# Four stages on one core: planes and pixels fetched from SBUF, first features made earlier, stores issued by SP, loops written out

## The reference

```python
x = x + _L0_conv_ref(_gn(x), w, b)        # 3x3 convolution, quantised
x = x + _L1_conv_ref(_gn(x), w1, w2)      # Fourier layer, 32x32 modes
x = x + _L2_conv_ref(_gn(x), cw, cb)      # 5x5 depthwise, filters pooled from the image
x = x + _L3_conv_ref(_gn(x), cw, ...)     # the layer that the change is about
```

```python
patches = _unfold(x, oh, ow)                        # 3x3 patches, (B, C, 3, 3, 128, 128)
x1 = patches.max(axis=1); x2 = patches.max(axis=2); x3 = patches.max(axis=3)
y = relu(bn(einsum('bihw,oi->bohw', concat([x1, x2, x3], 1), conv_w)))
out = mean(patches * y, over the 9 patch positions) # then pixel shuffle by 2
```

## Time and profile before

| | us |
|---|---|
| median of 3 runs | 3263.21 (3260.43 to 3278.74) |
| the profiled execution: time, span | 3277.86, 3276.0 |
| busy: PE, DVE, POOL, ACT | 2748.8, 2654.4, 1831.2, 1817.2 |
| fourth stage of image 0: first and last product on DVE | 589.61 to 931.04 |

### The profile page before, as it was taken

How to read it: one execution, slowest core, us unless ns; L and a number is a source line. 1 busy time by engine, 2 the same in 40 slices (tenths; PEclk the granted TensorE clock), 3 DMA queues, 4 the chain that set the end, 5 groups by cost and what they waited for, 6 DMA issues and landing times. The chain is left out here.

```text
span 3276.0 us, 45677 instructions
## 1 busy us (share of the span) xinstructions
PE 2748.8 (84%) x12765; PEld 2135.7 (65%) x12765; DVE 2654.4 (81%) x3575; ACT 1817.2 (55%) x2351; POOL 1831.2 (56%) x1296
## 2 busy tenths in 40 slices
PE   0087698899989779799989769889998977979998
PEld 0036586777747658577765658677775765857776
DVE  8986987788884888688888598778888489868887
ACT  7753655656552655566655265566655265556654
POOL 2013272799940446299990327279994044629998
PEclk9998899999997889899999689999999788989999
DMA  6732002899840200789880200289985020078984
GB/s 252 251 102 71 1 0 69 228 223 227 188 155 3 68 0 0 189 217 228 208 212 35 71 1 0 69 226 224 226 188 155 2 69 0 0 189 216 229 209 113
DMA packets 116199, 419.22 MB, mean 128 GB/s; under 512 B 16565, under 2 KB 30693, under 8 KB 105354
## 3 DMA queue, kind: packets, MB, share of 16 engines
q1 hardware_dynamic: 96058, 374.65, 44.5%
q10 hardware_dynamic: 18432, 38.54, 3.3%
q0 software_dynamic: 1616, 4.90, 0.5%
HBM read 340.57 MB, written 75.26 MB: 127 GB/s over the span
## 5 line engine op out<-in xcount | busy, mean ns | idle before, releaser
L920 POOL TENSOR_TENSOR work<-work 128x512 f32<-128x512 f32 x960 | 1283.3, 1342 | 411.0 <-DVE work L1340 310.4
L575 PE MATMUL psum<-workr,w 128*128 128x512 f32 (+1 forms) x5760 | 1366.0, 397 | 67.2 <-ACT workr L792 50.6
L575 PEld LDWEIGHTS psum<-workr,w 128*128 128x128 f32 (+1 forms) x5760 | 1085.9, 189 | 346.6 <-issue 51.4
L1331 DVE SCALAR_TENSOR_TENSOR work<-psum,work 128x512 f32<-128x512 f32 x1152 | 738.2, 679 | 34.0 <-POOL work L920 21.4
L544 PE MATMUL psum<-workr 128*128 128x512 f32 x2304 | 550.9, 401 | 21.5 <-DVE workr L1228 21.5
L894 POOL TENSOR_TENSOR work<-img 128x520 f32 (+1 forms) x256 | 387.7, 1545 | 283.7 <-DVE workr L1200 254.3
L544 PEld LDWEIGHTS psum<-workr 128*128 128x128 f32 x2304 | 439.7, 191 | 134.2 <-issue 24.7
L884 POOL TENSOR_TENSOR work<-work 128x1024 f32<-128x1024 f32 x40 | 112.9, 2856 | 479.1 <-DVE work L1113 479.1
L772 ACT CAST workr<-psum 128x650 fp32r<-128x650 f32 x128 | 90.0, 703 | 419.2 <-DVE psum L1307 419.2
L440 PE MATMUL psum<-work,taps 128*128 x1152 | 261.6, 391 | 44.4 <-DVE work L1064 44.4
L1304 DVE TENSOR_TENSOR psum<-psum,work 128x650 f32<-128x650 f32 x128 | 107.9, 843 | 208.4 <-ACT psum L765 208.2
(11 more groups left out here) (188 smaller groups left out, 3506.1 us busy)
## 6 DMA issues: line engine op xcount, KB each, us to landing
work<-gn_dram SPq DMA_DIRECT2D x256, 585.0 KB, 10.6
work<-gn_dram SPq DMA_DIRECT2D x256, 146.2 KB, 3.9
work<-gn_dram SPq DMA_DIRECT2D x128, 292.5 KB, 4.8
work<-in_x SPq DMA_DIRECT2D x16, 2048.0 KB, 7.3
img<-in_x SPq DMA_DIRECT2D x32, 1024.0 KB, 11.4
work<-in_mixw SPq DMA_DIRECT2D x64, 512.0 KB, 5.3
out_x<-work ACTq DMA_DIRECT2D x120, 256.0 KB, 6.2
gn_dram<-img SPq DMA_DIRECT2D x24, 1040.0 KB, 16.6
```

The lines of the kernel that those rows point to most:

```text
L575: mm = T.matmul(bank(m % 6), w5[wt][0:kr, P * n:P * n + P], ft[0:kr], start=(i == 0), stop=(i == 4))
L920: G.tensor_tensor(acc_t[v], acc_t[v], pd_t[(9 * v + n) % 6], ALU.add).then_inc(s_acc, 1)
L1331: V.scalar_tensor_tensor(out=tile4(pd_t[m % 6]), in0=tile4(psum[:, m % 6, :]), scalar=0.0, in1=rv[:, q, y0:y0 + RT, x0:x0 + WO], op0=ALU.m ...
```

## The change

- `gn_dram` and `store_rows` go. Planes and pixels are read from `img` in SBUF. A DMA takes one range of partitions on each side there, so the pixels are 16 DMAs of 32 partitions instead of 4 (`s_inr` counts 256 a pair instead of 64).
- SP issues the stores of tiles 0 to 29 in `load_next`: that of tile `2i` after the planes and ahead of maxima and pixels, that of tile `2i + 1` after the pixels. ACT's `store` goes. POOL still stores the last two tiles.
- The first tile's front part is made among the 32 reductions of `L1295` (DVE after reductions 20, 21 and 24, ACT ahead of its copies of the maxima), and PE's first products start ahead of the maxima; the transposed maxima go to PSUM bank 5 instead of 0.
- Every `Fori` inside an image (PE, ACT, POOL, DVE) is a Python `for`: the same instructions, written out, with constants in place of registers.

```diff
-                    sp.dma_start(a_t[k][0:32, :], gn_dram[0:32, n9]).then_inc(s_ab3[k], 16)
+                    sp.dma_start(a_t[k][0:32, :], img[0:32, n9]).then_inc(s_ab3[k], 16)
...
                 def load_pixels(u8, k):
-                    for n in range(4):
-                        sp.dma_start(r_t[k][32 * n:32 * n + 32, :].rearrange("p (q n) -> p q n", q=4),
-                                     byq[:, :, ds(u8 * PW, 9 * PW)]).then_inc(s_inr[k], 16)
-
-                def store_rows(e):
...
+                    for q in range(4):
+                        for n in range(4):
+                            sp.dma_start(r_t[k][32 * n:32 * n + 32, 9 * PW * q:9 * PW * (q + 1)],
+                                         img[32 * q:32 * q + 32, ds(u8 * PW, 9 * PW)]).then_inc(s_inr[k], 16)
+
+                def store(n):
+
+                    hold(sp, s_acc, b * NADDS + (n // 2 * ADDS + pool_adds(n % 2, 8) + 8))
+                    sp.dma_start(out[b, :, TILE * n:TILE * n + TILE], acc_t[n % 4]).then_inc(s_out[n % 4], 16)
 
                 def load_next(i):
 
                     p = i % 2
                     if i < NPAIR - 2:
                         if i % 2 == 0:
-                            hold(sp, s_gnd[i // 2 + 1], b * 16 + 16)
+                            hold(sp, s_gn3, b * NCH + (i // 2 + 2))
                         hold(sp, s_fmax, b * NT + (2 * i + 2))
                         load_planes(RP * (i + 2), p)
+                    store(2 * i)
                     hold(sp, s_pd, b * (9 * NT) + (18 * i + 18))
                     load_maxima(sp, RP * (i + 1), (p + 1) % 2)
                     load_pixels(RP * (i + 1), (p + 1) % 2)
+                    store(2 * i + 1)
...
                 for n in range(6):
+                    if n == 5:
+                        pe.wait_ge(s_mxz, b * 4 + 4)
+                        pe.wait_ge(s_mxl, b * 2 + 2)
                     product(n, n, terms, range(4))
...
-                with pe.Fori(1, NT // 4) as j:
+                for j in range(1, NT // 4):
...
+                act.wait_ge(s_tail, b * 32 + 16)
+                act.wait_ge(s_guard, b * 3 + 3)
+                prepare(0)
                 act.wait_ge(s_mxp, b * (NT + 1) + (NT + 1))
...
-                    store(j, 2 * p)
...
-                    store(j, 2 * p + 1)
...
+                for n in range(NT):
+                    v.wait_ge(s_mxp, b * (NT + 1) + (n + 1))
+                    V.tensor_reduce(mx_rq[:, RT * n:RT * n + RT, :],
+                                    psum[:, 2 + n % 4, :].rearrange("p (r q c) -> p r q c", r=RT, q=4), AX.X, ALU.max
+                                    ).then_inc(s_mxr, 1)
+                    if n in FIRST:
+                        front(0, 0, 0, FIRST.index(n))
```

More of the change, by code:

```diff
@@ L53 @@
 NW5 = 15
+FIRST = (20, 21, 24)
 MAXV = 127.0
@@ L399, in _ @@
                     load_next(i)
-                    if i % 2 == 1 and i // 2 + 3 < NCH:
-                        store_rows(i // 2 + 3)
+                for p in range(2):
+                    hold(sp, s_ab3[p], b * (96 * (NPAIR // 2)) + 96 * (NPAIR // 2))
+                    hold(sp, s_inr[p], b * (256 * (NPAIR // 2)) + 256 * (NPAIR // 2))
             for k in range(4):
@@ L429, in _ @@
             for b in range(B):
-                with pe.Fori(0, NCH) as e:
+                for e in range(0, NCH):
                     for v in range(4):
@@ L528, in _ @@
                 mm.then_inc(s_fsp, 1)
-                with pe.Fori(0, NBLK // 2) as j:
+                for j in range(0, NBLK // 2):
                     for p in range(2):
@@ L648, in _ @@
                         to_grid(e + 3)
-                with act.Fori(0, NT // 4) as j:
+                for j in range(0, NT // 4):
                     for k in range(2):
@@ L727, in _ @@
                 copy_third(0, 1)
-                with act.Fori(1, NBLK // 2 - 1) as j:
+                for j in range(1, NBLK // 2 - 1):
                     high2(j, 1)
@@ L798, in restore, with prepare @@
                                  ACT.Identity, bias=mom[:, 0:1], scale=std).then_inc(s_res, 1)
[L800 to L806, removed]
+                def prepare(k):
                     shifted(0, 0, k)
@@ L830, in step @@
                         side_low(jn, pn, 1)
-                    store(j, 2 * p + 1)
-                with act.Fori(0, NT // 4 - 1) as j:
+                for j in range(0, NT // 4 - 1):
                     step(j, 0)
@@ L900, in _ @@
                 hold(pool, s_x2, b * NT + NT)
-                with pool.Fori(1, NBLK // 2) as j:
+                for j in range(1, NBLK // 2):
                     for p in range(2):
                         transform(j, p)
-                with pool.Fori(0, NT // 4) as j:
+                for j in range(0, NT // 4):
                     for v in range(4):
@@ L1083, in _ @@
                 hold(v, s_link, link.base + link.n)
-                with v.Fori(0, NT // 4) as j:
+                for j in range(0, NT // 4):
                     for k in range(2):
@@ L1159, in _ @@
                     add_wave(0, k)
-                with v.Fori(1, NT // 8) as j:
+                for j in range(1, NT // 8):
                     for k in range(8):
@@ L1272, in _ @@
                 add_conv2(0, 1)
-                with v.Fori(1, NBLK // 2 - 1) as j:
+                for j in range(1, NBLK // 2 - 1):
                     low2(j, 1)
@@ L1353, in _ @@
                                 ALU.subtract).then_inc(s_mxl, 1)
-                for k in range(2):
-                    for step in range(3):
-                        front(0, 0, k, step)
+                for step in range(3):
+                    front(0, 0, 1, step)
                 pair(0, 0, first=True)
                 pair(0, 1)
-                with v.Fori(1, NPAIR // 2 - 1) as j:
+                for j in range(1, NPAIR // 2 - 1):
                     pair(j, 0)
```

56 lines of the change are left out of this document (21 added, 35 removed).

## The result

The changed kernel took 3703.33 us (median of 5, 3701.72 to 3725.56), the kernel before 3278.62 us (median of 5 in all, 3260.43 to 3278.74): a ratio of 1.1329, 95% interval 1.1287 to 1.1371 (the two medians alone would give 1.130). The profiled execution took 3725.56 us, with a span of 3723.7.

What follows compares the result with a forecast made beforehand. PE was taken as the bound, 21.28 us of a 21.6 us pair, with pixels only 3 us spare. 3277.9 + 426 - 8 - 2 = 3694 profiled; against the median 3263 + 416 = 3680 us, range 3490 to 3790.

Steps and rivals of the forecast that it cites:

- its own case: The prediction's main forecast for the whole kernel, given a chance of 0.65 and a range of 3615 to 3755 us.
- The store ahead of the pixels: Fourth stage, SP's queue: pixels wait behind a store, so a pair takes e + L, 28.7 us instead of 21.6; +426 us.
- e: Fourth stage: time from a pair's first product to the even tile's last (eighth) add; put at 14.4 us, first pair 13.7.
- L: Fourth stage: time from the even tile's last add to the next pair's last pixel landed; put at 14.3 us.
- issue-bound: Rival, chance 0.17: SP's DMA issues bound L in the fourth stage at 11.4 us; a pair 25.8, total 3505 us.
- Planes from SBUF, no `gn_dram`: Fourth stage: planes read from SBUF and the 8.65 MB of writes an image dropped; claimed 0 us in mid-stage.
- Earlier features: Start of the fourth stage: front steps cost +3.4 us, faster maxima give -5.4; net -2 an image, -8 in four.
- Stores off ACT: Fourth stage: ACT's stores hold up PE by 0.3 us a pair; this gain is lost in the longer wait, 0.
- Loops written out: Loops inside an image: writing them out gives 0 to -5 us, taken as -2.
- Slow clock: Rival, chance 0.06: PE, standing some 7.5 us a pair in the fourth stage, stays at 1.2 GHz; pair 35, total 4057 us.

Runs made afterwards that it cites:

- e12: The kernel before plus one wait: SP waits for the eighth add of the pair's even tile ahead of the next maxima and pixels; 3726.77 us, 1.1412.
- e1: The changed kernel with the pair's two stores back on ACT and none on SP; 3252.21 us, 0.9912.
- e4: The changed kernel with SP's queue reordered: odd tile's store of the preceding pair after half the pixel pieces, this pair's even tile's store after the rest; 3239.11 us, 0.988.
- e2: The kernel before with both stores on SP, where the change puts them, and none on ACT; 3723.19 us, 1.1365.
- e7: The changed kernel with POOL's adds of the fourth stage in their hardware loop again; 3682.2 us, 1.1281.
- e5: The changed kernel with the 16 pixel pieces reordered so that neighbours touch other partitions; 3607.19 us, 1.1048.
- e8: The kernel before with planes and pixels from `img`, in 6 and 16 DMAs, and no `gn_dram`; 3277.86 us, 1.0002.
- e10: The kernel before with the first tile's front part among the reductions and PE's and ACT's first steps ahead of the maxima; 3242.78 us, 1.002.
- e9: e4 with POOL's adds of the fourth stage in their hardware loop again; 3194.4 us, 0.9863.
- e3: The kernel before with every `Fori` inside an image written out as a `for`; 3286.42 us, 1.0028.
- e11: e4 with all 12 loops of the change as hardware loops again; 3199.33 us, 0.988.
- e6: The changed kernel with every pixel piece from pair 2 on cut to its first half, same 16 issues; 3581.59 us, 1.097.

## Why the prediction was right, and where its sizes were off

It gave 3680 us (3490 to 3790, its own case 3615 to 3755) and one mechanism; 3703 and that mechanism came.

- **The store ahead of the pixels**: right, and shown from both sides, by e12 (the wait alone brings it all) and by e1 and e4 (without it, or behind the pixels, it is gone). The term was +426 and is +497: a pair of 29.8 for 28.7, the first 29.4 for 28.0, the last 18.6 for 18.1.
- **e**: 14.4 was put, 14.9 measured. "Without registers 8 adds may win up to 0.4, and I take 0.3" has the wrong sign. With the loop in hardware e is 14.6 (e2, e7, e12), written out 14.9.
- **L**: 14.3 was put, 14.9 measured. The forecast paced it by the transfer alone, at 230 GB/s. That is only in part how it came: the issue was priced at 8.5 us for 18 DMAs from the rows of DMAs out of DRAM, and the store, the maxima and the 16 from `img` took 11.8. L is these issues and about 3 us to the last landing; the issue bound is 13.3 (e5), not 11.4, and the wait in the transfer is the 1.6 us above it. That L came within 0.6 us of the forecast is in part luck, as the transfer alone (e2) and the issues with their landing happen to take the same time. The rival *issue-bound* would have been a pair of 28.2, not 25.8.
- **The Trainium skill**, DMA: Bandwidth & Descriptors, section Bandwidth, has 435 GB/s as the bound for copies within SBUF. These pieces stay far below it: 221 GB/s with the engines busy at 0.96, and 246 interleaved with the engines busy at 0.94. Following the row was right.
- **Planes from SBUF, no `gn_dram`: 0** holds (e8, 1.0002).
- **Earlier features: -8** was too small: -19. The later of the two maxima DMAs lands after 5.3 us (12.4 before), not 7.1, and the gain needs the source too (e8, e10). The front steps cost what was put: the first of these DMAs is issued 28.2 us behind the stage's first transpose, 24.6 before.
- **Stores off ACT: the 0.3 us a pair are lost in the wait** holds, and e9, where SP stores behind the pixels, seems to have them: 21.3 us a pair.
- **Loops written out: -2** failed. Alone they cost 41 us in the fourth stage (e3), and in the changed kernel about 21 (e7), all on POOL: the prediction had looked for what a loop costs, not for what it hides. The third stage stayed as it was, 138.0 us against 137.8. Where POOL waits 8 us a pair, only the eight adds of e count, and the error stays small. It made the total worse by 21 us while the start's larger gain made it better by 11, so these two misses cancel in part.
- **Slow clock**: the clock fell, to 0.80 on average over the pair, and PE's 90 matmuls took 26.2 us, not 21.3, which shrank its hole to 3.6 us from the 7 put. At 26.2 of 29.8 it was not the bound: DVE's waits for PE grew by 9 us in the whole kernel (21.3 against 12.0).
- The sum against before without slow-clocked transforms: 3228 + 497 - 19 = 3706, and 3703 was measured. The forecast of 3680 stood on a median of 3263, which itself held about two such transforms, so a part of its nearness is luck too: the same +416 on 3228 would have been 3644.

## What to carry to other kernels

On an engine that issues DMAs in order, list for each wait what stands behind it and who is waiting for that. A store's wait for the end of a computation belongs behind every load whose buffer is already free: here the same two stores cost 13% ahead of the pixels and nothing that can be seen behind them (e11). Writing a loop out isn't free for an engine with two waits an instruction; look at the spacing of its operations, not at their duration. And a part that gives nothing alone may be half of a gain, so try pairs that free the two inputs of one start.

## What the runs showed of the hardware

- A written-out POOL add with a second wait starts every 1.434 us, in a hardware loop every 1.370, at the same duration of 1.29 us (medians 1294 and 1292 ns).
- SP's issue of a 32-partition pixel piece from `img` takes 0.64 to 0.67 us on average in e5, e6 and the changed kernel, mostly 0.59, with single ones above 1.3; in e1 and e8 the 16 take 12.1 to 12.2 us. The same six plane DMAs take SP 2.9 us from DRAM (before, from 629.43 on) and 5.2 from `img` (the changed kernel, from 3483.13 on).
- Sixteen copies in SBUF in an order in which neighbours touch other partitions move 246 GB/s instead of 221, and SP's issues pace them then. Which side's partitions matter wasn't tried.
- The 16 us steps by the granted clock of the second stage's transform. The transposes ahead of it run at 1.00 in both cases with PE equally busy. e1, with its loops written out, met it in none of 6 executions, and e11, with hardware loops, in none of 6 either, while before had 0 to 4 such images in one execution and its share differed from chip to chip. What decides it was not found.
